# A third buffer for the tile of x, and the largest weights spread by TensorE: a mixture-of-experts layer on one core

## The reference, cut to what matters

```python
def swiglu(x, w1, w2, w3):          # w1, w2: 256 x 512, w3: 512 x 256
    h = x @ w1
    return h * sigmoid(h) * (x @ w2) @ w3
gate_out = x @ gate_w               # 8 experts
top_v, top_i = top_k(gate_out, 2)   # and a softmax over the two
out = sum over experts of swiglu(x, ew1[e], ew2[e], ew3[e]) * w[e]
out = out + swiglu(x, sw1, sw2, sw3)
x = x + layernorm(out)
```

## Time and profile before

| | us |
|---|---|
| median of 3 runs | 872.01 |
| the runs | 872.02, 861.83, 872.01 |
| profiled execution, its own time | 865.95 |
| its span on the core | 864.2 |

### The profile page before, as it was taken

How to read it: one execution, slowest core, us unless ns; L and a number is a source line. 1 busy time by engine, 2 the same in 40 slices (tenths; PEclk the granted TensorE clock), 3 DMA queues, 4 the chain that set the end, 5 groups by cost and what they waited for, 6 DMA issues and landing times.

```text
span 864.2 us, 25172 instructions
## 1 busy us (share of the span) xinstructions
PE 778.7 (90%) x8205; PEld 553.5 (64%) x8205; DVE 549.9 (64%) x1180; ACT 442.3 (51%) x955; POOL 487.3 (56%) x625
## 2 busy tenths in 40 slices
PE   5689888898999994669999999999999999999991
PEld 5467767777877773346666666666666666666661
DVE  5888987997998994469643334343434343349893
ACT  3545555665666652224455555555555555445552
POOL 4133334876687776675399997666664333303342
PEclk9989989999999997699999999999999999999997
DMA  7423332443335346774111112222222221227984
GB/s 244 117 64 79 103 83 79 137 148 113 113 114 159 104 141 231 229 249 153 47 32 31 28 33 63 76 86 81 82 75 62 63 63 57 57 85 183 186 172 69
DMA packets 61404, 92.70 MB, mean 107 GB/s; under 512 B 7776, under 2 KB 43744, under 8 KB 61280
## 3 DMA queue, kind: packets, MB, share of 16 engines
q1 hardware_dynamic: 43840, 59.48, 24.3%
q0 software_dynamic: 11264, 23.23, 10.1%
q10 hardware_dynamic: 6176, 8.40, 3.2%
HBM read 59.20 MB, written 31.87 MB: 105 GB/s over the span
## 4 chain that ended last, share of the span: by engine, by line
PE 50%; DVE 3%; issue 3%; DMA 3%; POOL 1%; DVEq 1%; ACT 0%; POOLq 0%; SPq 0%; ACTq 0%
PE bank L1243 29%; PE bank L1253 14%; PE bank L1234 5%; PE bank L1228 3%; DMA xt<-xs_scratch 3%; DVEq L48 1%; DVE cmb L1403 1%; DVE cmb L1409 1%; DVE gg L1455 0%; DVE xl L1444 0%; POOL rsc L1507 0%; DVE state L914 0%; DVE stc L1414 0%; POOL x L593 0%; POOLq L1527 0%
## 5 line engine op out<-in xcount | busy, mean ns | idle before, releaser
L1243 PE MATMUL bank<-W,xh 128*128 (+1 forms) x832 | 250.9, 384 | 4.8 <-DVE xl L1444 3.4
L1437 DVE TENSOR_TENSOR gl<-bank,gh 128x512 f16<-128x512 f32 x104 | 71.8, 690 | 157.4 <-ACT gh L1293 154.1
L1243 PE MATMUL bank<-W,xl 128*128 (+1 forms) x416 | 159.2, 383 | 0.0
L1253 PE MATMUL bank<-W,gh 128*128 (+1 forms) x832 | 141.9, 273 | 1.1 <-DVE gl L1437 1.1
L1501 POOL DMA_INDIRECT yt_scratch<-ysh,dest x72 | 77.3, 1073 | 103.4 <-ACT ysh L1326 67.6
L1326 ACT ACTIVATE ysh<-bank,w_scale 128x256 f32<-128x256 f32 x104 | 49.2, 474 | 155.1 <-PE bank L1253 133.8
L1455 DVE SCALAR_TENSOR_TENSOR gg<-sl,w_scale,bank 128x512 f32<-128x512 f32 x104 | 77.6, 746 | 78.0 <-ACT sl L1311 60.2
L1243 PEld LDWEIGHTS bank<-W,xh 128*128 128x128 f16 x832 | 81.7, 99 | 60.9 <-issue 4.6
L1253 PE MATMUL bank<-W,gl 128*128 (+1 forms) x416 | 113.4, 273 | 0.0
L574 POOL DMA_INDIRECT xs_scratch<-xn_all,posi x64 | 90.9, 1421 | 27.8 <-issue 15.0
L1253 PEld LDWEIGHTS bank<-W,gh 128*128 128x128 f16 x832 | 81.4, 98 | 32.7 <-ACT ysh L1326 1.3
(11 more groups left out here) (183 smaller groups left out, 1363.7 us busy)
## 6 DMA issues: line engine op xcount, KB each, us to landing
W<-gate_scratch SPq DMA_DIRECT2D x64, 256.0 KB
xt<-xs_scratch SPq DMA_DIRECT2D x72, 130.0 KB
ysh<-yt_scratch SPq DMA_DIRECT2D x16, 512.0 KB, 4.5
W<-in_L_ffn_ew_dram ACTq DMA_DIRECT2D x15, 512.0 KB, 3.9
W<-in_L_ffn_ew_dram SPq DMA_DIRECT2D x9, 512.0 KB, 8.8
x_in<-in_L_attn_x_dram SPq DMA_DIRECT2D x16, 256.0 KB, 4.0
out_dram<-x SPq DMA_DIRECT2D x16, 256.0 KB
xs_scratch<-xn_all SPq DMA_DIRECT2D x16, 256.0 KB, 3.4
```

The lines of the kernel that those rows point to most:

```text
L1243: last = mm(dst[t.side][:, :], a[t.side][:, k, :], W16[:, e, m, s, k * H:(k + 1) * H], start=(n == 0), stop=(n == 3 * KC - 1))
L1253: last = mm(pYB[t.side][:, 0:D], a[t.side][:, c, :], W16[:, e, 2, s, c * D:(c + 1) * D], start=(n == 0), stop=(n == 3 * HC - 1))
L1437: V.tensor_tensor(gl[u.side][:, :, :].rearrange("p c t -> p (c t)"), pGT[:, :], gh[u.side][:, :, :].rearrange("p c t -> p (c t)"), ALU.sub ...
```

## The change

The tile of x gets three buffers (XT = 3), and SP's body t loads tile t+3. The spread of the largest weights no longer goes through DRAM: TensorE transposes the 128 x 7 largest values into one bank of PSUM, VectorE takes the largest per expert and forms a 7 x 7 diagonal matrix, TensorE multiplies it with ones, and VectorE computes the scales from the result in PSUM. This happens in bodies 9 and 10 (TURN = 9). The scans go from bodies 3 to 9 to bodies 2 to 8, the two functions for the tables share body 1, and ScalarE's loads of weights start in body -1. The transposes of x for tile 11, which write the same bank, wait for the scales.

```diff
+    XT = 3
-        def scales(link, dve, spread, first, end):
+        def scales(link, dve, largest, first, end):
...
-            dve.wait_ge(s_wall, 16 * (1 + int(first > 0)))
-            link(V.tensor_reduce(wmax[:, 1, at], spread[:, :, :].rearrange("p q e -> p e q"), AX_X, ALU.max))
-            link(V.tensor_scalar(wmax[:, 0, at], wmax[:, 1, at], 1e-30, None, ALU.max))
+            link(V.tensor_scalar(wmax[:, 0, at], largest, 1e-30, None, ALU.max))
...
-        spread_b = sc("spread_b", [P, P, NE - HEAD])
+        ones_f = sc("ones_f", [NE - HEAD, P])
+        wcol = sc("wcol", [NE - HEAD, 1])
+        wdiag = sc("wdiag", [NE - HEAD, NE - HEAD])
-        xt = [sc(f"xt{n}", [P, DX]) for n in range(2)]
+        xt = [sc(f"xt{n}", [P, DX]) for n in range(XT)]
...
-            peeled(-2, ENDS)
+            peeled(-XT, ENDS)
-        SHARE = 3 + NE - HEAD
+        TURN = EARLY - 3
# SP
-                if is_tile(t + 2):
-                    u = t + 2
+                if is_tile(t + XT):
+                    u = t + XT
...
-                    sp.dma_start(xt[t.side][:, 0:width], xs_d[bass.ds(row, P), 0:width]).then_inc(xt_loaded[t.side], 16)
-                if t.index == SHARE:
-                    share_largest(sp, spread_b, HEAD, NE)
+                    sp.dma_start(xt[t.index % XT][:, 0:width], xs_d[bass.ds(row, P), 0:width]).then_inc(xt_loaded[t.index % XT], 16)
# TensorE
-                due_dma(pe, xt_loaded, t)
+                need_dma(pe, xt_loaded, t.index)
...
+            def turn_largest():
+                pe.wait_ge(s_wmax, 1 + NE - HEAD)
+                nc.tensor.transpose(pT[0:NE - HEAD, D:D + P], wmax[:, 0, HEAD:NE], ident[:, :]).then_inc(T["largest_turned"], 1)
+
+            def spread_largest():
+                pe.wait_ge(T["largest_diag"], 1)
+                mm(pT[:, D + P:D + P + NE - HEAD], ones_f[:, :], wdiag[:, :], start=True, stop=True)\
+                    .then_inc(T["largest_all"], 1)
...
                 if is_tile(t + -1):
                     turn_g(t + -1)
+                if t.index == TURN:
+                    turn_largest()
+                if t.index == TURN + 1:
+                    pe.wait_ge(s_scale, 2)
                 if is_tile(t + 1):
                     turn_x(t + 1)
...
                     project(t + -2, e_before)
+                if t.index == TURN:
+                    spread_largest()
# ScalarE
-                for j in (2 * t.index, 2 * t.index + 1):
+                for j in (2 * t.index + 2, 2 * t.index + 3):
                     if 0 <= j < 3 * (NE - HEAD - AHEAD):
                         load_matrix(act, HEAD + AHEAD + j // 3, j % 3)
# VectorE
-            beside = [tiles_of_experts, expert_of_tiles, rows_of_tiles]
+            def diagonal():
+                rest = NE - HEAD
+                link(V.memset(ones_f[:, :], 1.0))
+                dve.wait_ge(T["largest_turned"], 1)
+                link(V.tensor_reduce(wcol[:, :], pT[0:rest, D:D + P], AX_X, ALU.max))
+                V.tensor_scalar(wdiag[:, :], ident[0:rest, 0:rest], wcol[:, :], None, ALU.mult)\
+                 .then_inc(T["largest_diag"], 1)
+
+            def scales_of_rest():
+                dve.wait_ge(T["largest_all"], 1)
+                scales(link, dve, pT[:, D + P:D + P + NE - HEAD], HEAD, NE)
+
+            def tables():
+                expert_of_tiles()
+                rows_of_tiles()
+
+            beside = [tiles_of_experts, tables]
             beside += [lambda e=e: largest_of(e) for e in range(HEAD, NE)]
-            beside += [lambda: None, lambda: scales(link, dve, spread_b, HEAD, NE)]
-            assert len(beside) == SHARE + 2
+            assert len(beside) == TURN
...
                      .then_inc(T["xl_ready"], 1)
+                    if t.index == TURN:
+                        diagonal()
...
                 if t.fixed and 0 <= t.index < len(beside):
                     beside[t.index]()
+                if t.index == TURN:
+                    scales_of_rest()
```

More of the change, by code:

```diff
@@ L1031, in prepare @@
                 if i == SPLIT:
-                    scales(link, dve, spread_a, 0, HEAD)
+                    dve.wait_ge(s_wall, 16)
+                    link(V.tensor_reduce(wmax[:, 1, 0:HEAD], spread_a[:, :, :].rearrange("p q e -> p e q"), AX_X, ALU.max))
+                    scales(link, dve, wmax[:, 1, 0:HEAD], 0, HEAD)
                     dve.wait_ge(s_scale, 1)
@@ L1117, in sandwich_kernel @@
         pT, pH1, pH2, pGT, pYB = bank[0], bank[1:3], bank[3:5], bank[5], bank[6:8]
-        namesB = ("late_chain pool_split experts_split xtT_done xh_ready xl_ready h1_done h2_done"
+        namesB = ("late_chain pool_split experts_split largest_turned largest_diag largest_all xtT_done xh_ready xl_ready h1_done h2_done"
                   " silu_ready gg_ready ggT_done gh_ready gl_ready y_done yo_ready tag_ready second_ready dest_ready").split()
         T = {n: sem("b_" + n) for n in namesB}
-        xt_loaded = [sem(f"xt_loaded{n}") for n in range(2)]
+        xt_loaded = [sem(f"xt_loaded{n}") for n in range(XT)]
         yt_stored = [sem(f"yt_stored{n}") for n in range(LANES)]
@@ L1225, in turn_x @@
             def turn_x(t):
-                due_dma(pe, xt_loaded, t)
+                need_dma(pe, xt_loaded, t.index)
                 for k in range(KC):
-                    last = nc.tensor.transpose(pT[:, k * P:(k + 1) * P], xt[t.side][:, k * P:(k + 1) * P], ident[:, :])
+                    last = nc.tensor.transpose(pT[:, k * P:(k + 1) * P], xt[t.index % XT][:, k * P:(k + 1) * P], ident[:, :])
                 last.then_inc(T["xtT_done"], 1)
+            def turn_largest():
[5 more added lines that the diff above has]
+                    .then_inc(T["largest_all"], 1)
             def turn_g(t):
@@ L1302, in body @@
                         e = expert_of(act, u)
-                        act.activation(tag[:, u.index - EARLY, 0:1], xt[u.side][:, D:D + 1], ACT.Copy)\
+                        act.activation(tag[:, u.index - EARLY, 0:1], xt[u.index % XT][:, D:D + 1], ACT.Copy)\
                            .then_inc(T["tag_ready"], 1)
-                        act.activation(tag[:, u.index - EARLY, 1:2], xt[u.side][:, D + 1:D + 2], ACT.Identity,
+                        act.activation(tag[:, u.index - EARLY, 1:2], xt[u.index % XT][:, D + 1:D + 2], ACT.Identity,
                                        bias=away9[:, e]).then_inc(T["tag_ready"], 1)
```

## The result

| | us, median | lowest to highest | runs |
|---|---|---|---|
| before | 863.04 | 854.49 to 872.02 | 20 |
| after | 868.02 | 857.77 to 876.53 | 20 |

The ratio of after to before is 1.0071, with a 95% interval of 1.0037 to 1.0106 (formed without disturbed runs, so it need not be the ratio of the two medians). The changed kernel is slower by 0.7%, about 6 us with 3 to 9 as bounds. That is inside 2%, but the interval excludes 1, and the forecast of a nil difference was wrong. The median of 868.02 meets the forecast's 868 by accident. The forecast started from a mean of four runs, 867.95, while the median of twenty is 863.04: the level was 5 us too high and the difference 6 us too small.

The account below looks back on a forecast made before the run. TensorE, busy 90% of the span, was taken as the bound, so only its waits could move. Terms -3.4 + 0.15 + 0 + 2.65 + 0.2 + 0.3 = -0.1 us on a mean of 867.95 gave 868 us, range 857 to 877.

Parts of the forecast that it names:

- The third buffer, -3.4: End of second phase, tiles 92 to 103: x loaded a tile earlier removes TensorE's waits for it, -3.4 us.
- The rival of DMA engines that bound the end: Tiles 92 to 103: DMA queueing keeps the period at 4.86, the 3.4 us are not had, 871.4 us; chance 0.13.
- Loads a body earlier, +0.15: Start of second phase: two weight-load issues ahead of ScalarE's first xh delay waiting TensorE, +0.15 us.
- The failed step: the spread by TensorE: Bodies 9 and 10: hand-over of the largest weights on TensorE's path, terms +2.65, +0.2 and +0.3 us.
- the wait for the last scan: Body 9: TensorE's new transpose waits for VectorE's scan of body 8, +2.65 us.
- The clock: Behind body 9's wait: no fall of TensorE's clock counted; its price would be about 2.5 us.
- The two small operations: Hand-over on TensorE: one added transpose and one matmul with few columns, +0.2 us (0 to 0.4).
- The wait for the scales: Body 10: TensorE holds tile 11's x transposes until VectorE has the scales, +0.3 us (0 to 1.5).
- The second step: merged tables at 0, with the stop as cover: Early second phase: both tables in body 1 cost 0, hidden by the stall near tile 4; uncovered 2.4 to 3.2 us.
- The stop: Near tile 4, all engines but GpSimd stall, some 8.6 us, tied to weight-load and scatter traffic; chance it goes 0.13.
- The last weights: Body 9: rival that expert 8's weights land late and hold the scan, 878.5 us at 22 us landing; chance 0.04.
- GpSimd's second split: After the scales: splits start about 8 us sooner, near 416 instead of 423.77, worth 0.

Follow-up runs that it names:

- after_again: The changed kernel, unchanged, measured in a second set: 869.5 us, ratio to before 1.0051.
- late_turn: The changed kernel with the hand-over of the largest weights (transpose, spread, scales) one body later: 865.54 us, ratio to before 0.9964.
- late_own: The changed kernel with the hand-over one body later and the spread in a PSUM bank of its own: 867.0 us, ratio to before 0.9981.
- memory_spread: The changed kernel with the largest weights spread through memory again, all else kept: 864.13 us, ratio to before 0.9954.
- the last set: Changed kernel, and it with memory spread, split tables or two x buffers, beside before at 849.52 us: ratios 1.0043, 0.9986, 1.0018, 1.0068.
- no_loads: The changed kernel with hand-over two bodies later, own spread bank, tables in two bodies, without 15 weight loads: 865.19 us, ratio to before 0.9888.

## Why the prediction was wrong

**The third buffer, -3.4: right.** E fell from 53.49 to 50.11 us, 3.38, and is 50.10 or 50.11 in every kernel with three buffers. The rival of DMA engines that bound the end fell with it: the busy share was 0.93 over the whole of E in after (the forecast had 0.96), TensorE didn't wait there at all, and neither ya nor the store came late enough to hold it.

**Loads a body earlier, +0.15: right.** Behind the copy of the logits the first matmul came after 348.49 to 354.95 = 6.46 us before and 351.84 to 358.45 = 6.61 after. It is 6.46 to 6.49 in every kernel without the earlier loads and 6.61 to 6.66 in every kernel with them.

**The failed step: the spread by TensorE**, forecast at 2.65 + 0.2 + 0.3 = 3.15 and measured at 5.30. Term by term: the wait for the last scan was 2.55 (forecast 2.65, right). The clock was counted at 0 and cost 3.63 - 1.94 = 1.69. The two small operations, at 0.2, cost 0.11 (from 414.97 to 415.08) + 0.32 (from 420.33 to 420.65), and 0.25 more that is left over in this body (the transposes of gg ahead of the wait took 0.63 us instead of 0.44, as TensorE ran empty), 0.68 in all. The wait for the scales was, by difference, 422.02 less the 415.08 + 4.55 + 1.69 + 0.32 = 421.64 at which the transposes would have come, 0.38 against 0.3. Together 5.30. The mis-sized term is the clock. The forecast had its price, 2.5 us, but not its place: it set a gap of 2.65 us nearer to the one of 1.34, behind which the clock had stayed, than to the one of 5.63, and counted no fall. At 2.55 us it fell in all five executions traced with that wait. Nor could two gaps have placed it: with the tables merged TensorE also waits some 2.2 us ahead of tile 3, and there the clock fell in two of eight executions (after_again, late_turn) and stayed in six. Here are the rows, and the windows of 4 us behind them, of after (1.00) and after_again (0.61):

```profile
375.21 0.61 PE L1253 MATMUL bank<-W,xh 128*128 128x512 f16 x2 [2.17 <-DVE xl L1475]
...
375.21:379.21 4.00, 4.00 (x25) 2.42 (x26) 4.00 (x3) 1.55 (x3) 2.88 (x3) 1.00 0.80 246
```

```profile
362.46 0.60 PE L1253 MATMUL bank<-W,xh 128*128 128x512 f16 x2 [2.22 <-issue]
...
362.46:366.46 4.00, 4.00 (x15) 2.12 (x16) 4.00 (x3) 2.03 (x4) 2.92 (x4) 0.61 0.58 187
```

So a gap of this size leaves it open whether the clock falls, and the fall belonged in the forecast as a case with its price. late_turn, late_own and memory_spread, which have no such wait, all have C at 29.5 to 29.8 and at most 0.3 us of loss.

The net loss in C is 4.3, not 5.3. Before has three bodies of 4.65, 4.85 and 4.84 us in this stretch, 0.7 in all over its usual pace, which in after lie inside the two long ones; another 0.3 is the first body of C, in which the stop's slow clock ends and which varies from 5.1 to 7.0 us.

**The second step: merged tables at 0, with the stop as cover.** With the stop, the step held as far as it can be seen. B is 34.55, 36.76, 36.06, 34.98 and 35.52 with the tables merged, mean 35.6, and 32.68, 35.64, 37.89, 32.79, 35.05 and 35.66 with the tables in two bodies, mean 35.0: 0.6 us apart within a spread of 5. The delay of tile 3 came as forecast, 2.17 us in the row above against 2.4, and the stop covers it: GpSimd's first split starts 30.6 to 30.9 us behind the end of A in all eleven of these traces, and the transposes of x for tile 6 come 3.9 to 6.2 us behind that with the tables merged and 1.9 to 7.3 with the tables in two bodies. Without the stop the work shows at 27.36 - 23.79 = 3.6 us. Of this, 0.5 lies between tiles 1 and 2, a body that varies from 4.5 to 5.9 us whatever the kernel; the other 3.0 (2.39 in the body of tile 3, 0.36 and 0.29 in the two that follow) are within the 2.4 to 3.2 that the forecast gave for a missing cover. How often an execution goes without the stop I can't say, so how much of these 3.6 us is in the measured 6 stays open.

**The sum with the measured terms**: -3.4 + 0.15 + 4.3 = +1.1 us with the stop, and up to 3.6 more without it, 4.7. The two ratios of after to before in sets with the stop say 6.1 (3.2 to 9.1) and 4.4 (1.1 to 7.6). The upper end of the sum lies in both; the lower lies outside the first and at the edge of the second. Yet every trace of before and after in these sets has the stop, which speaks for the lower end: by the ledger their traced executions are 2.5 us apart. In the last set, without the stop, the sum is -2.6 + 0.15 + 5.0 + 3.6 = 6.2 and the ratio says 3.7 (0.8 to 6.4). The sign, and the spread by TensorE as its cause, are shown by memory_spread against after; where the other 1 to 5 us of the first ratio lie is not.

**The stop** was taken for an effect of the traffic of weight loads. no_loads shows that it isn't. It goes with GpSimd's run of indirect DMAs: it ends within about 6 us of the last of them in every trace that has it, it shrinks when eight of them are taken out of the run (B from 35 to 30.4, 27.8 and 26.4), and a small one appears where the eight are put. Yet in the last set the same run of DMAs makes no stop at all. Why instructions that wait for TensorE's semaphores start late, and why only in some sessions, is not settled. The Trainium skill (Perfetto Trace Analysis, Per-instruction lifecycle) says that the propagation of a semaphore lies outside the window which the profiler reports for an instruction; no run here shows that this is what lasts so long, for elsewhere in the same trace TensorE starts 0.04 us behind VectorE's scan (414.93 to 414.97 in the chain above), while in the stop waits of 1 to 7 us have "remote" or "issue" as their releaser.

**The other rivals.** The last weights were not late: the scan of body 8 started at 411.57 right behind gg, so TensorE waited for VectorE and not for a load. GpSimd's second split started at 422.05, or 63.60 us behind the end of stretch A instead of 423.77 - 354.95 = 68.82: 5.2 us sooner where the forecast had about 8, since the hand-over itself was late. As forecast, nobody gained by it.

## What to carry to other kernels

A wait for another engine's side chain, put into TensorE's in-order stream, needs a body of slack. If it has none, count the wait and the clock behind it: here 2.55 us of waiting cost 4.2 with the slow clock and 5.3 with all that came with it, and one body later it cost next to nothing. Count work as free under a stall only if you know what makes the stall; otherwise its uncovered price belongs in the sum or at least in a likely case. And take the level from many runs: the forecast's four runs were off by as much as the whole effect.

## What the runs showed of the hardware

- TensorE's clock fell to its lower level behind a gap of 2.55 us in all five executions traced with that wait (a granted clock of 0.57 to 0.65 in the 4 us behind it), stayed behind one of 1.34 us, and did either behind waits of 2.17 to 2.32 us: it fell in two executions of eight. The Trainium skill (TensorE: Matmul & The Clock Gate, What's actually happening) says that the clock has two levels and none between; the trace agrees, as pairs of h1 matmuls took 0.59 us ahead of the wait and 1.06 behind it, and the one pair in between, in which the clock fell, 0.96.
- With a run of 12 indirect DMAs on GpSimd, 1.26 us apart, three other engines started late by 1 to 7 us each in all 11 traces with such a run ahead of the last set, and in none of the four of the last set, at a DMA share of 0.35 as well as of 0.77. How the one brings about the other is not shown.
- The first phase, nearly the same in all kernels, took 345 to 362 us. A ledger by stretches found differences of 0.1 us where the times of 12 runs had intervals of 3 us.
